# Two classes of landed scatters instead of four, and fewer stated waits, in the expert stage of an attention and routed-FFN kernel

## The chip, the cores and the metric

The kernel runs on 1 core of one Trainium2 chip. The metric is the device time of one execution in microseconds (us). The engines are PE (TensorE, matmuls), DVE (VectorE), ACT (ScalarE), POOL (GpSimd, which here issues the indirect DMAs) and SP (SyncE, which here issues all direct DMAs and does the waiting for them). They run side by side and meet only through semaphores: an instruction or a DMA adds to one, and another engine waits until it has reached a value.

## The reference

```
xn = layernorm(x)                                # x: 16 x 512 tokens of 256
out = x + attention(xn) + ffn(xn)
attention: Q, K = elu(xn Wq' + bq) + 1, elu(xn Wk' + bk) + 1;  V = xn Wv' + bv
           KV = K' V per batch;  context = Q KV / (Q . (sum K + 1e-6));  context Wo' + bo
ffn:       scores = sigmoid(xn gate');  group-limited top 4 of 16 experts, weights scaled by 2.5
           sum over the token's 4 experts of weight * (silu(xn up_e) @ down_e)
           + silu(xn shared_up) @ shared_down
```

So 8192 tokens go to 4 experts each: 32768 token rows, sorted by expert.

## The kernel before

Stage 1 goes over the 16 batches. It computes attention, the shared FFN and the routing, and POOL scatters each token's row into a table in DRAM, `rows_by_expert`. A row there has two halves of 272 words (`RW`): the first holds the normalised row and its weights, the second is the running sum that becomes the output.

Stage 2, the expert stage, works on `UNITS` = 143 units of 256 rows of one expert (`UR`), of which the last few are spare. Each unit goes through these steps, with the names that the rows show:

- SP, `load_rows` (L425): loads the unit's first halves into one of 8 buffers (parts of `xn` and `x_in`). It waits only for the buffer.
- SP, `load_sums` (L434 and L435): loads the second halves into `f_y` (part of `xn`), which other units may have written before. How many earlier units must have landed is known only at run time. The plan at the end of stage 1 (on DVE, `plan_rows`) writes it into a table: column 0 the first row, column 1 the expert, columns 2 to 1 + `CLS` the count for each class, one more for the first 8 units.
- PE, `turn_rows` (L1447): 4 transposes; ACT (L699) and DVE (L1246) split the result into a high and a low part (`xt_h`, `xt_l`).
- PE, up (L316, `bank_x`): 6 matmuls; ACT silu (L720, `hid`), ACT high part (L725, `hs_h`), DVE low part (L1269, `hs_l`).
- PE, down (L316, `bank_a` or `bank_y`): 6 matmuls; DVE (L1258) multiplies by the token's weight (`w`, L1243) and adds the sums.
- POOL (L575): two indirect DMAs of 128 rows scatter the unit's sums back, by the row numbers in `f_id` (L1252).

Each engine has one program order, written out by hand. SP alternates rows of unit u with sums of unit u - 3. PE does up(u), turn(u + 2), down(u - 1).

The classes count landed scatters. Scatters may land out of order, so unit u adds 32 (16 for each of its two DMAs) to semaphore `added[u % CLS]`, and POOL lets unit u's scatter start only once the last unit of the same class has landed: `adds_until(u - CLS)`. A count in a class is thus that of a known set of units. Before each load of sums SP waits for all classes in turn, each against a register. The registers come from the table by one load instruction per column for four units (`four_from`, L323), so every fourth unit has `CLS` such loads among its waits. Before the final copy (L452, 8 DMAs of 1024 KB from the table in DRAM to `out`) SP waits the same way (L447). `PRIMED` is the value that each class starts from: four scatters of batch 14 are counted on these semaphores instead of `scattered`.

ACT and PE wait for the engine that makes their input (`fx_done`, `fx_lo`, `fu_done`, `fs_done`) and, with `wait(...)`, for the last reader of the buffer that they overwrite.

Of the kernel before, what the change touches and what calls it, by code (L numbers as in the profile page):

```python
# [8 lines left out]
ALU = mybir.AluOpType  # L9
# [12 lines left out]
def attention_and_routed_ffn(  # L22
# [17 lines left out]
    B, S, D = x.shape  # L40
# [3 lines left out]
    SUB = S // P  # L44
# [20 lines left out]
    PW = D + 2  # L65
    XB = 3
    NB = 3
    CLS = 4
    COLS = 3 + CLS
    PACK = 6  # L70
    WORDS = -(-UNITS // PACK)
# [8 lines left out]
    with ExitStack() as ctx:  # L80
# [9 lines left out]
        def wait(eng, s, value):  # L90
            if value > 0:
                eng.wait_ge(s, value)
# [129 lines left out]
        u_class_i = sb("u_class_i", [P, CLS, 2], U32)  # L222
        u_class_n = sb("u_class_n", [P, CLS, 2], U32)

# [64 lines left out]
        scattered = [sem(f"scattered{i}") for i in range(NB)]  # L289
        added = [sem(f"added{i}") for i in range(CLS)]  # L290
# [9 lines left out]
        CONSTS = 12  # L300
        fours = {}
        BATCH_SCATTERS = 16 * SUB * TOP_K
        PRIMED = 16

        def scatters_until(c):
            return BATCH_SCATTERS * (c // NB + 1)
# [44 lines left out]
        def _(sp):  # L351
# [56 lines left out]
            sp.wait_ge(zeros_stored, 16 * len(zero_rows))  # L408
            sp.wait_ge(attn_ready, SUB * B)
            sp.wait_ge(scattered[(B - 3) % NB], scatters_until(B - 3))  # L410
            sp.wait_ge(scattered[(B - 2) % NB], scatters_until(B - 2) - 16 * CLS)
            for k in range(CLS):
                sp.wait_ge(added[k], PRIMED)

# [43 lines left out]
        def _(pool):  # L458
# [37 lines left out]
            def scatter_first(c, s):  # L496
                G.indirect_dma_start(  # L497
                    out=by_expert[:, :], in_=xn[:, c % NB, s, :], in_offset=None,
                    out_offset=bass.IndirectOffsetOnAxis(ap=slots_now[:, c % NB, s, 0:1], axis=0)
                ).then_inc(added[s] if c == B - 2 else scattered[c % NB], 16)  # L500

            pool.wait_ge(consts_made, CONSTS)
            inverse_root(0)
# [77 lines left out]
        def _(act):  # L581
# [113 lines left out]

            def rows_high(u):
                act.wait_ge(fx_done, u + 1)
                wait(act, fu_done, u - 3)
                S_.copy(f_h[u % 4], A[u % 2][:, :].rearrange("p (c s t) -> p c s t", c=KD, s=2)).then_inc(fx_hi, 1)  # L699

            act.wait_ge(plan_ready, 1)

            def stage(u):
                expert = expert_from(experts, u)
                wait(act, fu_done, u - 3)
                if u == 0:
                    act.wait_ge(c_done, SUB * B)
                    act.wait_ge(set_lo, SH + E)
                S_.copy(f_w[u % 4], we[:, bass.ds(expert, 1), :, 0:UPW].rearrange("p o a b -> p (o a) b")
                        ).then_inc(fw_ready, 1)  # L710
# [5 lines left out]
                rows_high(u)  # L716
            for u in range(UNITS):
                act.wait_ge(fu_done, u + 1)
                wait(act, fh_lo, u - 1)
                S_.activation(f_hid[u % 2], X[u % 2][:, 0:UR], ACT.Silu).then_inc(fs_done, 1)  # L720
                if u + 2 < UNITS:
                    rows_high(u + 2)
                act.wait_ge(fs_done, u + 1)
                wait(act, fd_done, u - 1)
                S_.copy(f_hh[u % 2], f_hid[u % 2]).then_inc(fh_hi, 1)  # L725
                if u + 2 < UNITS:
                    stage(u + 2)

        @block.vector
        def _(dve):  # L730
            V = nc.vector
# [355 lines left out]
            def plan_rows():  # L1087
                wide_u = [P, 2, B + 1, E - 1]
                V.tensor_scalar(u_tab[:, :, 1], u_ended[:, :], 0.0, None, ALU.max)
                V.tensor_tensor(u_before[:, :], u_first[:, :], u_units[:, :], ALU.subtract)  # L1090
                V.scalar_tensor_tensor(out=u_row[:, :], in0=u_in[:, :], scalar=float(UR), in1=u_base[:, :], op0=ALU.mult,
                                       op1=ALU.add)
                V.tensor_scalar(u_over[:, :], u_in[:, :], float(CAP // UR), 0.5, ALU.is_ge, ALU.mult)
                V.tensor_scalar(u_end_row[:, :], u_in[:, :], float(UR), float(UR), ALU.mult, ALU.add)
                plan(V.tensor_tensor(per_batch[:, :, :, 0:E - 1], mine[:, :, 0:E - 1].unsqueeze(2).to_broadcast(wide_u),
                                     so_far_at[:, :, 1:].unsqueeze(1).to_broadcast(wide_u), ALU.mult))
                planned()
                V.tensor_tensor(u_over[:, :], u_over[:, :], u_by[:, :], ALU.mult)
                V.tensor_reduce(u_other[:, :, :], per_batch[:, :, :, 0:E - 1], AX_X, ALU.add)
                plan(V.tensor_tensor(u_end_row[:, :], u_end_row[:, :], u_mine[:, :, B], ALU.min))  # L1100
                planned()
                V.tensor_tensor(u_row[:, :], u_row[:, :], u_fit[:, :], ALU.subtract)
                V.tensor_tensor(u_last[:, :], u_end_row[:, :], u_mine[:, :, B - 1], ALU.is_gt)
                V.scalar_tensor_tensor(out=u_pad[:, :], in0=u_units[:, :], scalar=float(UR), in1=u_other[:, :, B],
                                       op0=ALU.mult, op1=ALU.subtract)
                plan(V.tensor_tensor(u_below[:, :, :], u_mine[:, :, 0:B], u_end_row[:, :].unsqueeze(2)
                                     .to_broadcast([P, 2, B]), ALU.is_lt))
                planned()
                V.tensor_tensor(u_row[:, :], u_row[:, :], u_over[:, :], ALU.add)
                V.tensor_scalar(u_tab[:, :, 2 + CLS], u_last[:, :], float(BATCH_SCATTERS), float(scatters_until(B - 1 - NB)),  # L1110
                                ALU.mult, ALU.add)
                plan(V.tensor_tensor(u_below[:, :, :], u_below[:, :, :], u_other[:, :, 1:], ALU.mult))
                planned()
                V.tensor_tensor(u_row[:, :], u_row[:, :], u_real[:, :], ALU.mult)
                plan(V.tensor_reduce(u_need[:, :], u_below[:, :, :], AX_X, ALU.max))
                planned()
                V.tensor_tensor(u_tab[:, :, 0], u_row[:, :], u_spare[:, :], ALU.add)
                V.tensor_tensor(u_end[:, :], is_end[:, :], u_first[:, :], ALU.mult)
                plan(V.scalar_tensor_tensor(out=u_need_i[:, :], in0=u_need[:, :], scalar=UR - 1.0, in1=u_pad[:, :],
                                            op0=ALU.add, op1=ALU.add))  # L1120
                planned()
                plan(V.tensor_scalar(u_need_n[:, :], u_need_i[:, :], 8, None, ALU.logical_shift_right))
                planned()
                plan(V.tensor_tensor(u_before[:, :], u_before[:, :], u_need_n[:, :], ALU.add))
                planned()
                plan(V.tensor_tensor(u_before[:, :], u_before[:, :], u_real[:, :], ALU.mult))
                planned()
                plan(V.tensor_tensor(u_before[:, :], u_before[:, :], u_end[:, :], ALU.add))
                planned()
                for k in range(CLS):  # L1130
                    last = V.tensor_scalar(u_class_i[:, k], u_before[:, :], float(CLS - 1 - k), None, ALU.add)
                plan(last)
                planned()
                plan(V.tensor_scalar(u_class_n[:, :, :], u_class_i[:, :, :], 2, None, ALU.logical_shift_right))
                planned()
                V.tensor_scalar(u_tab[:, :, 2:2 + CLS].rearrange("p j k -> p k j"), u_class_n[:, :, :], 32.0, float(PRIMED), ALU.mult, ALU.add
                                ).then_inc(plan_made, 1)
# [137 lines left out]
        def _(pe):  # L1275
# [165 lines left out]

            def turn_rows(u):
                pe.wait_ge(rows_loaded[u % RB], 16 * (u // RB + 1))
                wait(pe, fx_lo, u - 1)
                for h in range(KD):
                    for tile in range(2):
                        last = T_.transpose(A[u % 2][:, (2 * h + tile) * P:(2 * h + tile + 1) * P],  # L1447
                                            f_rows[u % RB][:, tile, h * P:(h + 1) * P], ident[:, :])
                last.then_inc(fx_done, 1)
# [5 lines left out]
            for u in range(UNITS + 1):  # L1455
                if u < UNITS:
                    pe.wait_ge(fx_lo, u + 1)
                    pe.wait_ge(fw_ready, u + 1)
                    wait(pe, fs_done, u - 1)
                    split3(X[u % 2][:, 0:UR],  # L1460
                           [(f_w[u % 4][:, 0, h * I:(h + 1) * I], f_w[u % 4][:, 1, h * I:(h + 1) * I],
                             f_h[u % 4][:, h].rearrange("p s t -> p (s t)"),
                             f_l[u % 4][:, h].rearrange("p s t -> p (s t)")) for h in range(KD)]).then_inc(fu_done, 1)
# [43 lines left out]
```

## Time and profile before

| | |
|---|---|
| device time, median of 3 runs | 968.05 us (966.78 to 970.07) |
| span of the profiled execution, first to last instruction | 963.3 us |
| left around that span, if the execution was the median one | 4.75 us |
| expert stage: first load of rows issued | 466.9 us |
| final copy issued, and last of the span | 928.3 us, 963.3 us |

The page of the profile gives no total for the profiled execution beside its span, so its own time is taken as the span plus what lies around it. Busy time is the share in which an engine executes. In the lists, an idle time is put down to what ended it: a name of an engine and line is the instruction whose result came last; "issue" is that nothing in the profile was waited for; "remote" or "an unknown queue" is that no releaser was found that fits. SPq is SP's own instruction queue.

### The profile page before, as it was taken

The numbers are of one execution on the slowest core, as the hardware profiler recorded it, in microseconds if no ns is written. First come the engines' busy times: TensorE is split into PE (matmuls) and PEld (weight loads), VectorE is DVE, ScalarE is ACT, GpSimd is POOL, SyncE is SP. The second block draws the span as 40 slices with busy tenths as digits, with TensorE's granted clock in tenths as the row PEclk, the third lists the DMA queues.
The fourth block names the chain that finished last, engine by engine and source line by source line (L and its number), as shares of the span: only waits on it lengthen the run. The fifth ranks groups of instructions, "written<-read, shape, count | busy, mean of one in ns | idle before, by whom it ended". The sixth has DMA issues, their size and how long they took to land.

```text
span 963.3 us, 19900 instructions
## 1 busy us (share of the span) xinstructions
PE 763.9 (79%) x5264; PEld 698.6 (73%) x5264; DVE 700.5 (73%) x2390; ACT 551.7 (57%) x1142; POOL 579.7 (60%) x581
## 2 busy tenths in 40 slices
PE   5999999999999999996477676677767767677660
PEld 4899999999899988886366666666656657577660
DVE  6988988888888898889466566556565656666560
ACT  5777777676677766662255455455454554545450
POOL 1077766666777776666556565656565555556562
PEclk9999999999999999999599999989899898979895
DMA  5245554554444443333699798788878888798889
GB/s 160 88 157 193 187 181 175 188 193 182 149 160 181 147 135 118 119 113 117 193 288 285 237 283 254 240 265 261 248 234 281 272 246 272 234 273 252 261 263 311
DMA packets 142317, 202.16 MB, mean 210 GB/s; under 512 B 16176, under 2 KB 117184, under 8 KB 142208
## 3 DMA queue, kind: packets, MB, share of 16 engines
q1 hardware_dynamic: 114144, 116.47, 41.6%
q0 software_dynamic: 28064, 84.43, 22.9%
q8 instruction: 45, 0.74, 0.3%
q14 instruction: 64, 0.52, 0.2%
HBM read 104.19 MB, written 105.04 MB: 217 GB/s over the span
## 4 chain that ended last, share of the span: by engine, by line
PE 25%; issue 10%; DVE 7%; another core or an unknown queue 3%; ACT 2%; POOL 1%; SPq 1%; DVEq 1%; DMA 1%; POOLq 0%; ACTq 0%
PE bank_x L316 8%; PE bank_a L316 6%; PE bank_a L1447 6%; PE bank_y L316 5%; DVE xn L1258 3%; DVE hs_l L1269 2%; ACT xt_h L699 2%; DVE xt_l L1246 1%; DVE w L1243 0%; POOL rows_by_expert L575 0%; DMA xn<-rows_by_expert 0%; DVEq L1243 0%; POOL rows_by_expert L497 0%; SPq L323 0%
## 5 line engine op out<-in xcount | busy, mean ns | idle before, releaser
L575 POOL DMA_INDIRECT rows_by_expert<-xn,f_id x286 | 278.1, 972 | 196.2 <-issue 73.3
L491 POOL DMA_INDIRECT rows_by_expert<-xn,slots_now x192 | 196.7, 1024 | 123.1 <-PE bank_a L316 58.6
L1246 DVE TENSOR_TENSOR xt_l<-bank_a,xt_h 128x512 fp32r<-128x512 f32 x143 | 98.3, 687 | 113.7 <-ACT xt_h L699 96.0
L699 ACT CAST xt_h<-bank_a 128x512 fp32r<-128x512 f32 x143 | 83.8, 586 | 101.9 <-PE bank_a L1447 57.1
L720 ACT ACTIVATE hid<-bank_x 128x256 f32<-128x256 f32 x143 | 55.1, 385 | 123.9 <-PE bank_x L316 79.4
L316 PE MATMUL bank_a<-we,hs_h 128*128 x288 | 67.5, 328 | 68.3 <-DVE hs_l L1269 41.9
L316 PE MATMUL bank_y<-we,hs_h 128*128 x284 | 67.2, 330 | 65.9 <-DVE hs_l L1269 46.3
L316 PEld LDWEIGHTS bank_a<-we,hs_h 128*128 128x128 f32 x288 | 49.1, 206 | 82.0 <-issue 82.0
L316 PEld LDWEIGHTS bank_y<-we,hs_h 128*128 128x128 f32 x284 | 49.2, 209 | 79.4 <-issue 79.1
L316 PE MATMUL bank_y<-ws,hs_h 128*128 128x256 f32 x512 | 94.4, 282 | 1.4 <-DVE hs_l L998 1.4
L316 PE MATMUL bank_x<-xt_h,ws 128*128 128x512 f32 x256 | 92.1, 401 | 0.0
L497 POOL DMA_INDIRECT rows_by_expert<-xn,slots_now x64 | 80.3, 1254 | 17.9 <-issue 14.2
L316 PEld LDWEIGHTS bank_y<-ws,hs_h 128*128 128x128 f32 x512 | 80.9, 188 | 4.4 <-DVE hs_l L998 1.6
L316 PE MATMUL bank_y<-ws,hs_l 128*128 128x256 f32 x256 | 72.3, 282 | 0.0
L1258 DVE SCALAR_TENSOR_TENSOR xn<-bank_a,w,xn 128x256 f32<-128x256 f32 x144 | 62.6, 475 | 12.6 <-PE bank_y L316 7.3
L316 PE MATMUL bank_x<-xt_h,k_h 128*128 128x256 f32 x288 | 70.1, 304 | 0.5 <-issue 0.5
L316 PE MATMUL bank_x<-xt_h,k_l_p 128*128 128x256 f32 x284 | 68.1, 301 | 0.0
L1258 DVE SCALAR_TENSOR_TENSOR xn<-bank_y,w,xn 128x256 f32<-128x256 f32 x142 | 61.6, 474 | 3.9 <-PE bank_a L316 1.8
L652 ACT ACTIVATE k_f<-bank_a,minus_one 128x256 f32<-128x256 f32 x64 | 30.4, 474 | 57.6 <-issue 41.5
L1269 DVE TENSOR_TENSOR hs_l<-hid,hs_h 128x256 fp32r<-128x256 f32 x143 | 59.6, 416 | 1.3 <-issue 1.3
L725 ACT CAST hs_h<-hid 128x256 fp32r<-128x256 f32 x143 | 59.6, 417 | 0.1
L1447 PE MATMUL bank_a<-ident,xn 128*128 128x128 f32 x288 | 48.1, 295 | 10.4 <-DMA xn<-rows_by_expert 10.4
(289 smaller groups left out, 2418.7 us busy)
## 6 DMA issues: line engine op xcount, KB each, us to landing
xn<-rows_by_expert SPq DMA_DIRECT2D x215, 272.0 KB
x_in<-rows_by_expert SPq DMA_DIRECT2D x71, 272.0 KB
rows_by_expert<-spare SPq DMA_DIRECT2D x22, 544.0 KB
x_in<-in_L_attn_x_dram SPq DMA_DIRECT2D x16, 512.0 KB
out_dram<-rows_by_expert SPq DMA_DIRECT2D x8, 1024.0 KB
rows_by_expert<-xn,f_id POOLq DMA_INDIRECT x286
rows_by_expert<-xn,slots_now POOLq DMA_INDIRECT x256
w_raw<-in_L_ffn_expert_up_dram SPq DMA_DIRECT2D x32, 64.0 KB
```

The costliest lines, as they stand in the source:

```text
L316: last = nc.tensor.matmul(dst, a, b, start=start and k == 0, stop=stop and k == n - 1, skip_group_check=mixed)
L491: G.indirect_dma_start(out=half_rows[:, :], in_=xn[:, c % NB, s, 0:RW], in_offset=None, out_offset=bass.IndirectOffsetOnAxis(ap=slots_now[ ...
L497: G.indirect_dma_start(out=by_expert[:, :], in_=xn[:, c % NB, s, :], in_offset=None, out_offset=bass.IndirectOffsetOnAxis(ap=slots_now[:, ...
L575: G.indirect_dma_start(out=half_rows[:, :], in_=f_y[u % YB][:, tile], in_offset=None, out_offset=bass.IndirectOffsetOnAxis(ap=f_id[:, u % ...
L652: S_.activation(k_f[:, s, :], A[s][:, 0:D], ACT.Exp, bias=minus_one[:, 0:1])
L699: S_.copy(f_h[u % 4], A[u % 2][:, :].rearrange("p (c s t) -> p c s t", c=KD, s=2)).then_inc(fx_hi, 1)
L720: S_.activation(f_hid[u % 2], X[u % 2][:, 0:UR], ACT.Silu).then_inc(fs_done, 1)
L725: S_.copy(f_hh[u % 2], f_hid[u % 2]).then_inc(fh_hi, 1)
L1246: V.tensor_tensor(f_l[u % 4], A[u % 2][:, :].rearrange("p (c s t) -> p c s t", c=KD, s=2), f_h[u % 4].bitcast(F32), ALU.subtract).then_inc ...
L1258: last = V.scalar_tensor_tensor(out=y, in0=f_dn[u % 2][tile][:, 0:D], scalar=w2[:, u % 4, tile:tile + 1], in1=y, op0=ALU.mult, op1=ALU.add)
L1269: V.tensor_tensor(f_hl[u % 2], f_hid[u % 2], f_hh[u % 2].bitcast(F32), ALU.subtract).then_inc(fh_lo, 1)
L1447: last = T_.transpose(A[u % 2][:, (2 * h + tile) * P:(2 * h + tile + 1) * P], f_rows[u % RB][:, tile, h * P:(h + 1) * P], ident[:, :])
```

## The change

Four things are edited.

`CLS` goes from 4 to 2. With it the table has 5 columns instead of 7, `PRIMED` is 32 instead of 16, unit u adds to `added[u % 2]`, and POOL's scatter of unit u waits for unit u - 2 to have landed instead of u - 4. SP waits for 2 classes per unit instead of 4 and loads 2 count columns per four units instead of 4.

ACT loses four waits per unit: for `fu_done` ahead of `rows_high` and of `stage`, for `fh_lo` ahead of the silu, for `fd_done` ahead of `hs_h`. PE loses two: for `fx_lo` ahead of the transposes and for `fs_done` ahead of up. No compute instruction and no DMA is added or taken away.

```diff
-    CLS = 4
+    CLS = 2
-        PRIMED = 16
+        PRIMED = 16 * SUB // CLS
@@ sync
-            sp.wait_ge(scattered[(B - 2) % NB], scatters_until(B - 2) - 16 * CLS)
+            sp.wait_ge(scattered[(B - 2) % NB], scatters_until(B - 2) - 16 * SUB)
@@ gpsimd, scatter_first
-                ).then_inc(added[s] if c == B - 2 else scattered[c % NB], 16)
+                ).then_inc(added[s % CLS] if c == B - 2 else scattered[c % NB], 16)
@@ scalar
             def rows_high(u):
                 act.wait_ge(fx_done, u + 1)
-                wait(act, fu_done, u - 3)
             def stage(u):
                 expert = expert_from(experts, u)
-                wait(act, fu_done, u - 3)
...
                 act.wait_ge(fu_done, u + 1)
-                wait(act, fh_lo, u - 1)
                 S_.activation(f_hid[u % 2], X[u % 2][:, 0:UR], ACT.Silu).then_inc(fs_done, 1)
...
                 act.wait_ge(fs_done, u + 1)
-                wait(act, fd_done, u - 1)
                 S_.copy(f_hh[u % 2], f_hid[u % 2]).then_inc(fh_hi, 1)
@@ vector, plan_rows
-                plan(V.tensor_scalar(u_class_n[:, :, :], u_class_i[:, :, :], 2, None, ALU.logical_shift_right))
+                plan(V.tensor_scalar(u_class_n[:, :, :], u_class_i[:, :, :], CLS.bit_length() - 1, None,
+                                     ALU.logical_shift_right))
@@ tensor
             def turn_rows(u):
                 pe.wait_ge(rows_loaded[u % RB], 16 * (u // RB + 1))
-                wait(pe, fx_lo, u - 1)
...
                     pe.wait_ge(fw_ready, u + 1)
-                    wait(pe, fs_done, u - 1)
```

On SP, at the first loads of sums of the expert stage (L323 loads a table column into registers, the ISA rows of L435 wait and form the address), the order changes so, with - for before and + for now:

```order
 L323 TENSOR_LOAD q_f [waits added0]
-L323 TENSOR_LOAD q_f [waits added1]
-L323 TENSOR_LOAD q_f [waits added2]
-L435 ISA [waits added3]
+L435 ISA [waits added1]
 L435 DMA xn<-rows_by_expert 128x2x272
 L323 TENSOR_LOAD q_f x2
 L425 ISA [waits scattered0]
 L425 DMA x_in<-rows_by_expert 128x2x272
-L435 ISA [waits added0,added1,added2,added3]
+L435 ISA [waits added0,added1]
 L435 DMA xn<-rows_by_expert 128x2x272
```

Two table loads with their waits have gone from every fourth unit, and two bare waits from each of the others; all DMAs stand where they stood.

On POOL, at the scatters of units 2 and 3, before:

```order
L575 DMA rows_by_expert<-xn,f_id 237568x272 [waits added2,fd_done,id_ready,y_ready]
L575 DMA rows_by_expert<-xn,f_id 237568x272 [waits fu_done]
L575 DMA rows_by_expert<-xn,f_id 237568x272 [waits added3,fd_done,id_ready,y_ready]
L575 DMA rows_by_expert<-xn,f_id 237568x272 [waits fu_done]
L575 DMA rows_by_expert<-xn,f_id 237568x272 [waits added0,fd_done,id_ready,y_ready]
```

and now:

```order
L575 DMA rows_by_expert<-xn,f_id 237568x272 [waits added0,fd_done,id_ready,y_ready]
L575 DMA rows_by_expert<-xn,f_id 237568x272 [waits fu_done]
L575 DMA rows_by_expert<-xn,f_id 237568x272 [waits added1,fd_done,id_ready,y_ready]
L575 DMA rows_by_expert<-xn,f_id 237568x272 [waits fu_done]
L575 DMA rows_by_expert<-xn,f_id 237568x272 [waits added0,fd_done,id_ready,y_ready]
```

The order is the same; the wait for a landed scatter now names the unit two before.

## Rows read from the trace of the kernel before

**Rows 1.** The page: the span.

```profile
span 963.3 us, 19900 instructions
```

**Rows 2.** Windows: expert stage, and final copy alone. Columns are in the first line.

```profile
core 0: us, PE busy (x) PEld busy (x) DVE busy (x) ACT busy (x) POOL busy (x), PEclk, DMA share, GB/s
484.00:925.00 441.00, 309.08 (x2161) 282.49 (x2162) 271.58 (x809) 228.96 (x540) 260.74 (x268) 0.93 0.84 259
...
943.00:963.00 20.00, 0.00 (x0) 0.00 (x0) 0.00 (x0) 0.00 (x0) 3.80 (x4) 0.50 0.98 306
```

**Rows 3.** Waits 484 to 925 us: who waited for whom, total, times, longest.

```profile
ACT xt_h L699 <- PE bank_a L1447: 55.6, 35, 2.5
...
ACT xt_h L699 <- remote: 36.4, 16, 3.9
...
PEld bank_a L1447 <- DMA xn<-rows_by_expert: 1.7, 1, 1.7
PE bank_a L1447 <- DMA xn<-rows_by_expert: 1.5, 1, 1.5
PEld bank_a L1447 <- DMA x_in<-rows_by_expert: 0.9, 2, 0.5
```

**Rows 4.** The chain of waits, 472 to 493 us: start, us, what ran.

```profile
475.72 0.30 SPq L323
476.12 0.30 SPq L323
476.50 0.30 SPq L323
...
479.19 0.37 SPq L435
479.82 0.37 SPq L425
480.67 0.37 SPq L435
...
482.64 0.69 SPq L424
...
485.23 0.30 SPq L323
...
487.77 4.41 DMA xn<-rows_by_expert
492.22 0.66 PE bank_a L1447 x4
```

**Rows 5.** Waits of SP's queue, 484 to 925 us.

```profile
SPq L434 <- DMA rows_by_expert<-xn,f_id: 22.0, 19, 3.6
SPq L323 <- DMA rows_by_expert<-xn,f_id: 6.4, 3, 2.9
```

**Rows 6.** Timeline of SP's DMAs at the end: start, us, what.

```profile
919.14 0.01 SPq L435 DMA_DIRECT2D xn<-rows_by_expert  x1
...
928.29 25.02 SPq L452 DMA_DIRECT2D out_dram<-rows_by_expert  x8
```

**Rows 7.** SP's waits between 919 and 923 us.

```profile
SPq L323 <- DMA rows_by_expert<-xn,f_id: 2.4, 1, 2.4
```

**Rows 8.** Timeline of POOL, three places; in brackets the idle time before.

```profile
710.22 1.13 POOL L575 DMA_INDIRECT rows_by_expert<-xn,f_id  x1 [0.30 <-issue]
...
714.18 0.96 POOL L575 DMA_INDIRECT rows_by_expert<-xn,f_id  x1 [0.30 <-issue]
...
916.90 0.96 POOL L575 DMA_INDIRECT rows_by_expert<-xn,f_id  x1 [0.30 <-issue]
```

**Rows 9.** Timeline of PE and ACT between 563 and 567 us.

```profile
563.40 1.05 PE L1447 MATMUL bank_a<-ident,x_in 128*128 128x128 f32 x4
...
566.52 0.59 ACT L699 CAST xt_h<-bank_a 128x512 fp32r<-128x512 f32 x1 [1.87 <-remote]
```

## The prediction

> **What bounds the kernel now.** I read four views, in this order. First the windows, because the change touches one stage only. Between 484 and 925 us [rows 2] POOL issues 268 scatters, two per unit, so 134 units pass in 441 us, 3.29 us each. No engine is near full in it: PE 309, DVE 272, POOL 261, ACT 229 of 441 us. The 16 DMA engines are busy 0.84 of the time.
>
> Second the waits of that stretch. ACT stands 55.6 us before it splits the turned rows because of PE's transposes, and another 36.4 us with no releaser found [rows 3]. An example of the latter: the four transposes stand at 563.40 and take 1.05 us, and ACT's next split starts only at 566.52 [rows 9]. What is nearly absent is a wait for loaded rows: PE and its weight queue waited 1.7, 1.5 and 0.9 us for them, 4.1 us together. So in the middle of the stage the ring PE, ACT, DVE, PE sets the pace, and SP's loads come ahead of it.
>
> Third the chain of waits at the start of the stage [rows 4]. There it is different. From 475.72 to 487.77 us the chain runs through SP alone (L323, L434, L435, L425), then through the landing of the rows of unit 8 (4.41 us), and only at 492.22 us reaches PE. In these 12 us the kernel does wait for SP's instructions.
>
> Fourth SP's queue. In the middle it waited 22.0 and 6.4 us for landed scatters, 22 times [rows 5]; at the end its last load of sums stands before the first part of the final copy, which starts at 928.29 us [rows 6]. From there to the end of the span, 963.3 us [rows 1], are 35 us, with the DMA engines at 0.98 in the last 20 of them and nothing else going on but 4 scatters [rows 2]. The final copy is bound by the DMA engines; it moves with its start.
>
> **The change part by part.**
>
> SP at the start of the stage. One table load with its wait costs 0.39 us: the loads stand at 475.72, 476.12 and 476.50 [rows 4]. A bare wait costs 0.07 us: from one DMA to the next it is 0.63 us with one wait between them (479.19 to 479.82) and 0.85 us with four (479.82 to 480.67), so 0.22 us for three [rows 4]. Ahead of the rows of unit 8 stand the sums of units 0 to 4. Units 0 and 4 have table loads: two pairs less each, 4 x 0.39 = 1.56 us. Units 1 to 3 lose two bare waits each, 6 x 0.07 = 0.44 us. Together 2.0 us, all on the chain. From below: the rows before unit 8 shift by 0.8 to 1.2 us only, and if the ring has become the bound already at unit 6 or 7, 1.2 us are left; the landing of 4.41 us may grow by what the loads are closer together. From above: some of SP's steps are longer, as the wait at 482.64 with 0.69 us [rows 4]; if one of the removed steps is such a one, it is 2.7 us. I take 2.0 and keep 0.5 to 2.7.
>
> About the table load the Trainium skill ("DMA: Bandwidth & Descriptors", section "Latency and other measured facts") gives a floor of about 600 ns. The trace shows 0.30 us for three of them [rows 4], so here the trace decides against the page; by the page's figure the four pairs would bring 2.7 us instead of 1.56, an estimate, and the sum would be 1.1 us lower.
>
> SP in the middle. Every four units lose two pairs and six bare waits, 0.78 + 0.44 = 1.2 us, so 134 units about 41 us of SP's time. Cover: the loads come ahead of the ring, and the wait for rows is 4.1 us in all [rows 3]. More than these 4.1 us can't come back directly. I take 0; the time turns into longer waits of SP for landed scatters. Indirectly SP's DMAs shift against the scatters and against the ring; 55.6 + 36.4 us of ACT's waits [rows 3] hang on how such things meet. A twentieth of that, 4.6 us either way, is my estimate of what this may do; I take 0.
>
> SP at the end. The last load of sums waits for a landed scatter eight units back, then come the waits of that unit (four table waits, one of them behind it) and four more before the copy. Two and two of them go, 4 x 0.07 = 0.3 us, on the path, because the copy starts right behind. At least 0.1, at most 1.1 us if the two table loads of the unit two before count as well.
>
> The waits of ACT and PE. Their conditions are true long before: ACT waits for PE or executes most of the time, and what its queue handles meanwhile costs nothing. ACT executes 229 / 134 = 1.7 us of each 3.29 us, PE 2.3 us, so their queues run ahead. The trace does not show the price of such a wait on the path; one per unit at SP's 0.07 us would be 134 x 0.07 = 9 us, none is 0. A loss is excluded, since nothing is issued in their place. I take 0, because before the split ACT idles by whole microseconds [rows 9], and keep 9 as the far end.
>
> The plan on DVE has two small instructions less, some tenths of a microsecond, while POOL still scatters batch 15, which the rows loads wait for. I take 0.
>
> The added wait on POOL. Unit u's scatter now needs unit u - 2 landed. Behind it on POOL stand only later scatters; for them SP waits, 8 units later at most, and for SP the sums of DVE. What a landing takes: SP issued at 919.14 and then waited 2.4 us for the scatter of the unit eight before, whose second DMA stands at 916.90 [rows 6 to 8]. So it landed at 921.55, 4.65 us after its issue. What there is: a unit takes 3.29 us, a pair 6.58 us, less 0.96 + 0.30 us between its two scatters [rows 8], so 5.3 us on average from the second scatter of u - 2 to the first of u. At a tight place it is 3.96 us (710.22 to 714.18) [rows 8]. So on average 0.65 us are to spare, and at tight places POOL starts up to 0.7 us later. POOL has room: 2.5 us of each 3.29 us. The delay reaches only sums that are loaded well ahead. From below 0. From above: should it lengthen each of the 22 waits of SP by 0.7 us, 15 us of waiting, less than the 41 us that SP has won. I take 0 on the path.
>
> The same page of the Trainium skill ("Anatomy of one DMA — SWDGE (gpsimd) path") puts a DMA of this path at 2.0 us plus bytes over 436 GB/s and puts most of the 2 us down to the receipt of the write. For 128 rows of 1088 bytes that is 2.3 us, an estimate, and by it the new wait would never bite. The trace shows twice that, 4.65 us, under load; the sum stays the same by either, but the second makes the wait a real risk.
>
> Sum: 963.3 - 2.0 - 0.3 = 961.0 us of span; with 4.75 us around it 965.75, and since some of the 2.0 us may be swallowed by the ring, I say 966.0 us. The median of the runs shown is 968.05 us, so this is 2 us or 0.2% less.
>
> **The rivals.**
>
> B, SP's relief reaches the path. For it: a wait of SP can stand 0.69 us where others take 0.07 [rows 4], and a queue with fewer instructions is late more seldom. Against it: only 4.1 us of waits for rows [rows 3]. All of them and the start: 966.0 - 4.1 = about 962 us; with one hidden wait of ACT on some units, 961.5 us.
>
> C, the wait on POOL takes over, and the kernel becomes slower. A pair of units can't be faster than 1.27 us plus the landing. At 4.65 us that is 5.9, under 6.58 us. It decides from a landing of 5.3 us on average. At 5.4 us it would be (1.27 + 5.4 - 6.58) / 2 x 134 = 6 us, so 972 us. For it: the DMA engines are at 0.84, and loads issued earlier lie closer to the scatters; in short fast stretches the wait bites already at 4 us. Against it: 0.65 us of spare and loads of sums far ahead.
>
> D, the start brings nothing, since the ring would have waited a few units later anyway: 968 us. For it: the chain changes from SP to the ring just there.
>
> **How the numbers follow.** A measurement of this kernel tells about 0.3%, 2.9 us, from no change. The forecast (A, 966.0 us, its own range 963.5 to 968.5) has 0.45, of which about a third lies below 965.15 us. B has 0.20, all faster. C has 0.18, slower. D has 0.17, mostly no change. That makes faster 0.39, no change 0.41, slower 0.20. The range from 957 us (the 9 us of the hidden waits) to 972.5 us takes in B and the middle of C and leaves out about 0.15.
>
> **What would show it.** Right: the chain between 475 and 492 us is about 2 us shorter, and PE turns the rows of unit 8 near 490.2 us; 72 table loads and 286 waits less on SP; SP's waits for landed scatters grow from 28 us to 40 or more; the middle keeps 3.29 us per unit; the final copy starts 2 to 2.5 us earlier and still takes 35 us. B: a middle below 3.26 us per unit, and no waits for rows at all. C: POOL's idle time put down to a landed scatter of its own (none is there before), with more than 3.32 us per unit. D: PE's turn of unit 8 earlier, but unit 12 at the old time. Wrong altogether I would be if the waits of 55.6 and 36.4 us changed by more than a tenth, for which I have no mechanism.

## The result, and the profile after

The changed kernel takes 975.86 us (median of 17 runs, 966.47 to 980.90), the kernel before 966.31 us (17 runs, 965.22 to 970.07) on the same chip: a ratio of 1.0084, 95% interval 1.0066 to 1.0103. It is slower by 0.8%, where 966.0 us and most likely no loss were forecast; 975.86 us lies outside the range of 957 to 972.5 us. The profiled execution took 980.90 us, the longest of the 17, so the rows below show somewhat more of the loss than the median has.

The page and the windows of the kernel after; the windows answer to [rows 1] and the first of [rows 2]:

```profile
span 978.4 us, 18974 instructions
...
core 0: us, PE busy (x) PEld busy (x) DVE busy (x) ACT busy (x) POOL busy (x), PEclk, DMA share, GB/s
484.00:925.00 441.00, 311.97 (x2122) 283.58 (x2121) 267.99 (x794) 226.45 (x532) 253.93 (x262) 0.90 0.81 253
...
484.00:780.00 296.00, 214.04 (x1471) 193.08 (x1470) 185.19 (x550) 156.69 (x368) 169.85 (x176) 0.92 0.81 254
```

POOL issues 262 scatters in these 441 us instead of 268: 441 / 131 = 3.37 us per unit in place of 3.29. 134 units x 0.08 is 10 us. That is the size of the loss between the medians, 9.6 us. The span of this execution is 15.1 us longer; of that 2.1 us are there before the stage begins (its first load of rows is issued at 469.0 us instead of 466.9) and 2.0 us lie in the final copy, so 11 us fall in the stage. By POOL's own starts the first scatter of unit 4 comes 5.3 us later than before (499.8 instead of 494.5 us) and that of unit 135 12.5 us later (937.7 instead of 925.2): 3 us are lost in the first units and 7 us in the 131 after them.

The waits of the same stretch, answering to [rows 3], with one of POOL that before did not have at all:

```profile
ACT xt_h L698 <- PE bank_a L1443: 35.4, 25, 3.1
POOL rows_by_expert L575 <- DMA rows_by_expert<-xn,f_id: 31.9, 19, 3.0
...
ACT xt_h L698 <- remote: 23.2, 16, 2.5
...
PEld bank_a L1443 <- DMA xn<-rows_by_expert: 15.6, 9, 5.0
PE bank_a L1443 <- DMA xn<-rows_by_expert: 13.8, 8, 4.8
...
PEld bank_a L1443 <- DMA x_in<-rows_by_expert: 9.6, 9, 1.9
```

POOL now stands 31.9 us for landed scatters of its own, and PE stands at loaded rows, which [rows 3] showed with 1.5 us. SP's queue, answering to [rows 5], went from 28 to 113 us of waits for landed scatters:

```profile
SPq L434 <- DMA rows_by_expert<-xn,f_id: 105.7, 58, 7.1
SPq L323 <- DMA rows_by_expert<-xn,f_id: 7.4, 3, 4.8
```

The end, answering to [rows 6], is a timeline of SP's DMAs (start, us, what):

```profile
941.40 23.07 SPq L452 DMA_DIRECT2D out_dram<-rows_by_expert  x8
```

The final copy starts 13.1 us later than before and takes 37.0 us to the end of the span instead of 35.0. At the start of the stage, SP's loads of rows for units 4 and 8 and PE's turns of both; first SP, then PE:

```profile
479.29 0.37 SPq L425 DMA_DIRECT2D x_in<-rows_by_expert  x1
...
485.61 1.12 SPq L425 DMA_DIRECT2D xn<-rows_by_expert  x1
```

```profile
484.05 0.60 PE L1443 MATMUL bank_a<-ident,x_in 128*128 128x128 f32 x4
...
495.93 1.05 PE L1443 MATMUL bank_a<-ident,xn 128*128 128x128 f32 x4
```

And the same four places of the kernel before, SP and PE:

```profile
478.34 0.37 SPq L425 DMA_DIRECT2D x_in<-rows_by_expert  x1
...
481.50 0.66 PE L1447 MATMUL bank_a<-ident,x_in 128*128 128x128 f32 x4 [0.41 <-DMA x_in<-rows_by_expert]
```

SP does get from unit 4 to unit 8 in 6.3 us instead of 9.4 (478.34 to 487.77 [rows 4]), 3.1 us sooner, where 2.0 were forecast. PE does not: 11.9 us between its turns instead of 10.7 (481.50 to 492.22 [rows 4]). The rows of unit 8 no longer hold PE (there is no idle time before its turn now), and something else does. Relative to the first load of rows of the stage, PE turns unit 12 at the same time in both, after 36.5 us before and 36.2 us now.

### The profile page after: what moved, and what is told of

Same layout as the page of the kernel before. It is cut to its first block, busy times and chain, and to the rows that moved or that the text cites. A ratio compares the mean times of both kernels' runs of the same rounds, so it can differ in the third digit from the quotient of the medians.

```text
span 978.4 us, 18974 instructions
## 1 busy us (share of the span) xinstructions
PE 770.0 (79%) x5264; PEld 702.8 (72%) x5264; DVE 701.5 (72%) x2388; ACT 553.0 (57%) x1142; POOL 577.6 (59%) x581
## 4 chain that ended last, share of the span: by engine, by line
PE 16%; issue 11%; DVE 9%; DMA 6%; another core or an unknown queue 3%; ACT 3%; POOL 2%; DVEq 1%; POOLq 0%; SPq 0%; ACTq 0%
PE bank_x L316 5%; DMA rows_by_expert<-xn,f_id 5%; PE bank_a L316 4%; PE bank_y L316 4%; DVE xn L1255 4%; PE bank_a L1443 3%; DVE hs_l L1266 3%; DVE xt_l L1243 1%; DMA xn<-rows_by_expert 1%; POOL rows_by_expert L575 1%; ACT xt_h L698 1%; ACT hid L717 1%; DVE w L1240 1%; ACT hs_h L721 1%
## 5 line engine op out<-in xcount | busy, mean ns | idle before, releaser
L316 PE MATMUL bank_a<-we,hs_h 128*128 x288 | 70.5, 338 | 57.9 <-DVE hs_l L1266 51.2
L316 PEld LDWEIGHTS bank_a<-we,hs_h 128*128 128x128 f32 x288 | 51.7, 217 | 71.5 <-issue 71.5
L1443 PE MATMUL bank_a<-ident,xn 128*128 128x128 f32 x288 | 50.9, 306 | 27.4 <-DMA xn<-rows_by_expert 26.4
L316 PE MATMUL bank_x<-xt_h,k_l_p 128*128 128x256 f32 x284 | 70.3, 308 | 0.0
L1443 PEld LDWEIGHTS bank_a<-ident,xn 128*128 128x128 f32 x288 | 37.8, 157 | 31.0 <-DMA xn<-rows_by_expert 29.5
```

Source lines behind the costliest of these rows:

```text
L316: last = nc.tensor.matmul(dst, a, b, start=start and k == 0, stop=stop and k == n - 1, skip_group_check=mixed)
```

## The experiments

They ran on other chips than the first comparison, and there the kernel before takes 855 to 857 us, not 966. Each was run beside the kernel before on its own chip, and ratios are against that. The times are medians of 4 to 12 executions.

| label | us | ratio to before, 95% interval | us per unit, 484 to 780 us |
|---|---|---|---|
| e1_waits_only | 855.78 | 0.9992 (0.9978 to 1.0006) | 2.55 |
| e2_cls2_only | 963.81 | 1.1235 (1.1190 to 1.1280) | 3.38 |
| e3_gate2 | 951.98 | 1.1119 (1.1089 to 1.1148) | 3.25 |
| e4_sp_padded | 948.65 | 1.1086 (1.1056 to 1.1116) | 3.23 |
| e5_gate3 | 865.21 | 1.0098 (1.0082 to 1.0115) | 2.64 |
| e6_gate1 | 1242.96 | 1.4514 (1.4491 to 1.4537) | 5.24 |
| e7_after_again | 965.98 | 1.1242 (1.1198 to 1.1285) | 3.36 |
| e8_sums3_before | 855.46 | 0.9981 (0.9970 to 0.9993) | 2.55 |
| e9_ring_before | 856.90 | 1.0010 (0.9997 to 1.0024) | 2.54 |
| e10_ring_after | 970.45 | 1.1307 (1.1268 to 1.1346) | 3.40 |
| e11_sums3_after | 963.04 | 1.1236 (1.1210 to 1.1262) | 3.40 |
| e12_ring2_before | 940.73 | 1.1000 (1.0970 to 1.1030) | 3.15 |
| e13_ring2_after | 968.69 | 1.1324 (1.1288 to 1.1360) | 3.33 |

The last column is 296 us over half the count of POOL's scatters in the windows. The three kernels e1, e2 and e3 cut the change into its parts.

**e1_waits_only**: the kernel before without the six waits.

```
-                wait(act, fu_done, u - 3)      (twice)
-                wait(act, fh_lo, u - 1)
-                wait(act, fd_done, u - 1)
-                wait(pe, fx_lo, u - 1)
-                    wait(pe, fs_done, u - 1)
```

> The kernel before, with only the six waits of ACT and PE taken out; four classes stay. Theory G (the wait of POOL's scatter for the unit two before is the cause): as before, 966.3 us, within 2 us, POOL never waits for a landed scatter, SP's waits for landed scatters stay near 28 us. Rival W (without these waits ACT and PE run in another rhythm and this costs the time): as the changed kernel, near 976 us. Rival S (SP's shorter instruction stream costs the time): 966.3 us, like G.

Ratio 0.9992: the six waits are worth nothing that can be measured, with 2 us as the far end of the interval. Its windows row is the measure for what the stage can do on such a chip:

```profile
484.00:780.00 296.00, 253.10 (x1856) 225.18 (x1855) 230.48 (x697) 208.12 (x464) 225.34 (x232) 0.98 0.99 329
```

The DMA engines are at 0.99 and carry 329 GB/s. POOL is at its limit too: it starts 232 scatters in 296 us, and in no run do two scatters start less than 1.26 us apart (0.96 us busy and 0.30 us between), so 232 x 1.26 = 292 of the 296 us are POOL's own spacing. Over units 4 to 135 POOL idles 0.5 us in all beyond these 0.30 us. So on such a chip the ring of engines does not set the pace; POOL's scatters fill 2.53 of the 2.55 us per unit. Neither limit was relieved by itself, so what the DMA engines alone would allow is not known.

**e2_cls2_only**: the changed kernel with the six waits put back, so `CLS = 2` alone.

> The changed kernel with the six waits of ACT and PE put back; two classes. Theory G: as the changed kernel, 973 to 979 us, POOL waits some 30 us for landed scatters and SP 100 us or more. Rival W: back to 966 us. Rival S: 973 to 979 us, like G.

963.81 us, 12.4% over before on its chip: two classes alone bring the loss, so rival W falls. G and S are left.

**e3_gate2**: the kernel before, four classes, SP's program untouched, and one wait more for POOL.

```
                 pool.wait_ge(added[u % CLS], adds_until(u - CLS) if u >= CLS else PRIMED)
+                if u >= 2:
+                    pool.wait_ge(added[(u - 2) % CLS], adds_until(u - 2))
```

> The kernel before, with four classes, the same stream of SP and all waits of ACT and PE; POOL alone waits in addition until the scatter of the unit two before has landed. Theory G: 973 to 979 us, the whole loss, with the lag from a unit's sums to its scatter growing from about 2 to 8 us and SP's waits for landed scatters near 100 us. Rival S: 966 us, since SP's stream is the old one. Rival W: 966 us. If G and S share the loss: 970 us.

952 us: POOL's wait for unit u - 2 alone brings 95 of the 107 us that two classes cost. SP's lighter program, the plan and the classes themselves play no part in these 95 us. The row of its windows beside that of e1:

```profile
484.00:780.00 296.00, 216.55 (x1474) 199.61 (x1475) 190.48 (x554) 164.61 (x369) 176.78 (x182) 0.90 0.83 258
```

**e4_sp_padded**: the changed kernel, but SP loads each of the two count columns twice and waits on each class twice, so that its program is about as long as before.

```
-                for k in range(CLS):
-                    sp.wait_ge(added[k], four_from(..., 2 + k, u, ...))
+                for i in range(2 * CLS):
+                    k = i % CLS
+                    sp.wait_ge(added[k], four_from(..., 2 + k, u, ..., copy))
```

> The changed kernel, in which SP loads each count column twice and waits for each class twice per unit, so that its instruction stream is as long as before; two classes and POOL's wait for the unit two before stay. Theory G: as the changed kernel, 973 to 979 us; SP's waits for landed scatters shorter than 116 us by up to 40 us, since SP comes to them later. Rival S (the shorter stream lets SP's loads collide with the scatters): back to 966 to 968 us.

948.65 us, 15 us faster than e2: the instructions taken from SP cost time instead of bringing any. e3, with SP's full program too, is 12 us faster than e2. So rival S is not what brings the 95 us, but a shorter program of SP adds 12 to 15 us to them.

**e5_gate3 and e6_gate1**: as e3, with u - 3 and with u - 1 in place of u - 2.

> The kernel before, with one wait added: POOL's scatter of unit u also waits for the scatter of unit u-3. Theory G (distance): the two units between leave 2 x 2.56 - 1.26 + 2.56 = 6.4 us from the second scatter of u-3 to the first of u at the pace of the kernel without the wait (2.56 us per unit in the stage), against a landing of about 3.7 us and 0.9 us from landing to start, 4.6 us; so nearly free: within 1% of before, under 866 us where before takes 857. Rival H (any wait of POOL for a landed scatter costs, whatever its distance, since POOL's queue is held by it): about as slow as with u-2, 950 us.

> The kernel before, with one wait added: POOL's scatter of unit u also waits for the scatter of unit u-1, so each unit's two scatters go alone. Theory G: a unit can't be faster than 1.27 us (first scatter to second, and on) less nothing, plus a landing of 3.7 us after the second scatter's start, plus 0.9 us: about 0.96 + 3.7 + 0.9 = 5.5 us a unit against 2.56, 140 units, so about 857 + 410 = 1270 us; at the least 1150 us if the landing falls to 2.8 us because the DMA engines are less busy. Rival H: like the wait for u-2, 950 us.

865 and 1243 us, close to what the distance theory gave (under 866, 1270), and far from its rival's 950. The cost goes by the distance and not by having a wait. e6 shows the wait bare, in its chain of waits (start, us, what):

```profile
607.83 0.99 POOL rows_by_expert L577
608.82 0.30 issue
609.13 2.44 DMA rows_by_expert<-xn,f_id
611.57 0.02 issue
611.59 0.04 POOLq L570
611.63 0.04 issue
611.68 0.04 POOLq L574
611.72 0.73 issue
612.45 0.95 POOL rows_by_expert L577
```

The reader sees two pieces. From the start of the second scatter (607.83) to its landing (611.57) are 3.7 us. Then POOL's queue has the news at once (L570), but its next scatter starts only at 612.45, 0.88 us after the landing. That second piece is what the forecast left out. The profile's spans on POOL are rough, so where exactly a scatter starts, and with it the split into the two pieces, is less sure than their sum.

**e7_after_again**: the changed kernel itself on such a chip.

> The changed kernel itself, beside the others on their chip. If the six removed waits are worth nothing here as well, it takes what the two classes alone took on such a chip, 960 us within 8 us, 11 to 13% over before where before takes 857 us. If the chip is like the first one (before at 966 us), it takes 976 us, 0.8% over.

965.98 us, 12.4% over before. Its POOL timeline (start, us, what, idle time before) has a pattern:

```profile
602.26 0.96 POOL L575 DMA_INDIRECT rows_by_expert<-xn,f_id  x1 [1.50 <-DVE f_id L1249]
603.52 0.96 POOL L575 DMA_INDIRECT rows_by_expert<-xn,f_id  x1 [0.30 <-DMA rows_by_expert<-xn,f_id]
604.79 1.19 POOL L575 DMA_INDIRECT rows_by_expert<-xn,f_id  x1 [0.31 <-issue]
606.28 0.96 POOL L575 DMA_INDIRECT rows_by_expert<-xn,f_id  x1 [0.30 <-issue]
609.06 0.96 POOL L575 DMA_INDIRECT rows_by_expert<-xn,f_id  x1 [1.81 <-DVE f_id L1249]
...
615.89 0.95 POOL L575 DMA_INDIRECT rows_by_expert<-xn,f_id  x1 [2.08 <-DVE xn L1255]
...
622.68 0.96 POOL L575 DMA_INDIRECT rows_by_expert<-xn,f_id  x1 [2.05 <-DVE xn L1255]
```

Four scatters, two units, go close together, then POOL idles 1.5 to 2.1 us until the first unit of the group has landed. The groups start at 602.26, 609.06, 615.89 and 622.68: 6.8 us for two units. The releaser named is mostly DVE's `f_id` or `xn`, and it is the wrong one: by the semaphore events the landing of u - 2 comes 0.86 us ahead of the start, at each of the four. e1 at the same place has no such gaps, and its scatters stand 1.27 us apart without end:

```profile
600.01 0.96 POOL L575 DMA_INDIRECT rows_by_expert<-xn,f_id  x1 [0.30 <-DVE f_id L1248]
601.27 0.96 POOL L575 DMA_INDIRECT rows_by_expert<-xn,f_id  x1 [0.30 <-issue]
602.53 0.96 POOL L575 DMA_INDIRECT rows_by_expert<-xn,f_id  x1 [0.30 <-DVE f_id L1248]
603.80 0.96 POOL L575 DMA_INDIRECT rows_by_expert<-xn,f_id  x1 [0.30 <-PE bank_y L316]
```

So a rule can be written: distance d in units, time for them = 1.26 (first to second scatter) + L (start of the second scatter to its landing) + 0.88. The table takes units 4 to 135 from the semaphore events, those whose scatter starts under 1.05 us after the landing that it waits for:

```
kernel           d  such units  mean L  by the rule, us  measured  rule / d  all units
e6_gate1         1  132 of 132   3.12     5.26             5.30      5.26      5.30
e3_gate2         2   91 of 132   4.32     6.46             6.49      3.23      3.26
e4_sp_padded     2   84 of 132   4.26     6.40             6.45      3.20      3.25
e2_cls2_only     2   73 of 132   4.50     6.64             6.68      3.32      3.36
e7_after_again   2   72 of 132   4.63     6.77             6.77      3.39      3.37
e5_gate3         3   34 of 132   5.82     7.96             8.04      2.65      2.65
```

The measured time of such units agrees with the rule by construction, since they were picked by the third piece. The test is in the last two columns: the rule over d against the pace of all these units, from the start of unit 4 to that of unit 135. They differ by 0.05 us at most. With d = 2 the units that are not in the count are nearly all the second of a group, which follows at once.

The idle time agrees too. What POOL idles beyond 0.30 us ahead of these units is 103 us in e7, 96 in e2 and 86 in e3, where the kernels lose 109, 107 and 95 us. The granted clock is no rival: it is 0.93 in e7 and 0.98 in e1, but e12 and e13 below have 1.00 and 0.99 and still differ by 28 us.

Why a lighter SP makes it worse is not shown. The landings that are waited for take 4.50 to 4.63 us in e2 and e7 and 4.26 to 4.32 in e3 and e4, but they are picked by being waited for: over all units the means are 4.13 and 4.13 against 4.10 and 4.08 us, hardly apart.

**e11_sums3_after**: the changed kernel with `SUMS_AHEAD = 3`. Does the lateness need SP's queue to reach PE?

> The changed kernel (966 us on such a chip) with SP loading the sums three units ahead in place of four, so that it needs a scatter one unit older to have landed. Theory Q (a scatter that starts late after its wait makes SP stand at the load of sums, with the loads of rows behind it, and PE then waits for the rows): with 3.4 us more room the waits of PE for rows shrink, and the unit goes from 3.37 us toward the bound of the pair, (1.26 + 4.15 + 0.86) / 2 = 3.14 us: 935 to 955 us. Rival R (the pair alone bounds it, and SP's queue adds nothing): 960 to 970 us, no change. Against both, sums that come late for DVE: over 975 us.

963.04 against 965.98 us, 1.1236 against 1.1242 by the kernel before on each one's chip: R, no change. The waits only changed place. First e7, then e11, waits from 484 to 780 us:

```profile
PEld bank_a L1443 <- DMA xn<-rows_by_expert: 57.0, 36, 4.2
...
DVE f_id L1249 <- DMA xn<-rows_by_expert: 23.8, 28, 2.8
```

```profile
DVE f_id L1249 <- DMA xn<-rows_by_expert: 80.0, 69, 4.2
...
PEld bank_a L1443 <- DMA xn<-rows_by_expert: 16.9, 15, 3.1
```

PE's waits for rows fall and DVE's for sums rise, at the same pace. They are followers of POOL's pair and not a cause; I had taken them for one.

**e8_sums3_before**: the same in the kernel before, with the six waits out.

> The kernel before with four classes, the six waits of ACT and PE out, and SP loading the sums three units ahead in place of four, so SP waits for a scatter of unit u-5+... one unit younger is no longer asked for so early: SP stood 60.2 us in 55 waits of 3.7 us at line 434 in the variant with four. Theory Q (those waits hold back the loads of rows and weights queued behind, and so PE): with 2.56 us more room each, most of the 60 us of waits go, and a part reaches the end: 840 to 852 us where before takes 857. Rival (DMA engines at 0.99 bound the stage anyhow): 855 to 860 us, no change. Against both, if the sums then come late for DVE: over 865 us.

Ratio 0.9981, interval 0.9970 to 0.9993. Theory Q falls here too: POOL's scatters already stand 1.27 us apart with no idle time beyond the 0.30 us but 0.2 us in all, so there is nothing behind SP's waits to win. It is the only kernel of the study whose whole interval lies below 1, by 1 to 2 us, less than the 0.3% that count here.

**e9, e10, e12 and e13**: why only 0.8% on the first chip? The pace before was 3.29 us per unit there and 2.55 here. These four slow the ring on purpose: ACT does each of its two casts per unit twice (e9 from the kernel before, e10 from the changed one) or three times (e12, e13), the extra ones into tiles that nobody reads.

```
+                S_.copy(q_h[:, u % 2, :], A[u % 2][:, :])
                 S_.copy(f_h[u % 4], ...).then_inc(fx_hi, 1)
...
+                S_.copy(q_l[:, u % 2, 0:UR], f_hid[u % 2])
                 S_.copy(f_hh[u % 2], f_hid[u % 2]).then_inc(fh_hi, 1)
```

> The kernel before, with the ring PE, ACT, DVE, PE made slower: ACT copies each unit's turned rows and its hidden rows twice (first to tiles that nobody reads), 0.59 + 0.41 = 1.0 us more per unit. In the variant with the six waits out a unit takes 2.56 us in the stage, of which ACT executes 2.0. All theories: ACT alone then needs 3.0 us per unit, the ring 3.0 to 3.6; so 857 + 138 x (0.45 to 1.0) = 920 to 995 us, 960 as a guess. It stands in for the first chip, where the kernel before took 3.29 us per unit.

> The changed kernel with the same two extra copies of ACT per unit. Theory M (the slower of the two limits counts, ring or POOL's wait for unit u-2, and on the first chip the ring had already used up the time): only 0 to 3% over the kernel before with the same copies, where without the copies it is 12.4% over. Rival N (the losses add, and the first chip differs in how much the wait itself costs): 11 to 12% over it, some 107 us more, 1065 us.

856.90 us: my expectation for e9 was wrong. The second cast of each kind costs nothing, since ACT still fits into the 2.54 us that POOL's scatters take per unit. So this pair told nothing about M and N, except that the loss stayed at 13%. The larger dose:

> The kernel before, with each of ACT's two casts per unit done three times (twice to tiles that nobody reads). With two each, ACT was busy 280 of 296 us in the stage, 2.42 us per unit, and the time stayed 857 us: the ring had more room than thought. One more of each is 0.64 + 0.47 = 1.1 us, so 3.5 us per unit, ACT the bound in all theories: 857 + 138 x (3.5 - 2.55) = 988 us, 970 to 1000. With that the kernel before has about the pace that it had on the first chip (3.29 us per unit) or is a little slower.

> The changed kernel with the same six casts per unit. Theory M (the slower limit counts; where something else has already taken the pace to 3.3 us or more per unit, POOL's wait for u-2 costs little, as on the first chip with 0.8%): 0 to 3% over the kernel before with the same casts. Rival N (the losses add; the first chip differs in the wait itself): 10 to 12% over it, 107 us or so.

The windows of e12 and then of e13:

```profile
484.00:780.00 296.00, 199.85 (x1501) 177.97 (x1500) 200.43 (x560) 296.00 (x752) 179.06 (x188) 1.00 0.85 266
```

```profile
484.00:780.00 296.00, 200.31 (x1464) 176.82 (x1462) 197.64 (x548) 290.34 (x733) 171.81 (x178) 0.99 0.81 251
```

In e12 ACT never stands, 296.00 of 296 us, and bounds the stage at 3.15 us per unit. That is less than the 3.5 expected, and the time of 940.73 us less than 970 to 1000, because casts that follow each other overlap. ACT's timeline in e12 (start, us, what):

```profile
599.50 1.47 ACT L699 CAST q_h<-bank_a 128x512 fp32r<-128x512 f32 x1
599.99 1.48 ACT L700 CAST xr_h<-bank_a 128x512 fp32r<-128x512 f32 x1
600.46 1.49 ACT L701 CAST xt_h<-bank_a 128x512 fp32r<-128x512 f32 x1
600.94 1.32 ACT L727 CAST q_l<-hid 128x256 fp32r<-128x256 f32 x1
601.25 1.32 ACT L728 CAST xr_l<-hid 128x256 fp32r<-128x256 f32 x1
...
602.66 1.49 ACT L699 CAST q_h<-bank_a 128x512 fp32r<-128x512 f32 x1
```

Each is recorded with 1.3 to 1.5 us, but they start 0.48 and 0.31 us apart, so a further pair costs 0.79 us and not 1.1; the unit is 3.16 us (599.50 to 602.66). The same count gives e9 3.15 - 0.79 = 2.36 us of ACT per unit, under the 2.54 that POOL's scatters take.

With the change the time is 968.69 us, 28 us or 3.0% more and not 109 us. M holds and N falls: the slower of two limits counts. The pace of the changed kernel is 3.33 to 3.40 us per unit in all its forms but the padded one (3.23); what it costs is the distance from the pace before to that. The pace before on the fast chips is taken from e1, as the kernel before was not profiled there. 134 units x (3.36 - 2.55) = 109 us on the fast chips (965.98 - 856.56 = 109.4 measured), x (3.33 - 3.15) = 24 us behind ACT (28.0 measured), x (3.36 - 3.29) = 9 us on the first chip (9.6 measured; by the starts of units 4 and 135 the pace is 3.34 there, which gives 7 us).

## Why the prediction was wrong

**The step that failed** is "The added wait on POOL ... I take 0 on the path". Landing was put at 4.65 us, room at 5.3 us, so 0.65 us to spare. What was missing is the 0.88 us between landing and the next scatter's start, seen in e6. With it 5.53 us stand against 5.3, nothing is to spare, and rival C's own formula gives (1.27 + 4.65 + 0.88) / 2 = 3.40 us per unit against 3.29: 134 x 0.11 = 15 us, so 981 us. Measured are 975.86. Rival C was the right mechanism with one term too few, and got 0.18.

That this sum comes so near is in part luck. The 4.65 us was one landing. The landings that were waited for average 4.63 us in e7, but over all its units the mean is 4.13, and 4.13 + 0.88 us would still have fitted into 5.3.

The same step held that a late scatter reaches only sums that are loaded well ahead. That was the second fault. Room ahead covers a delay that comes now and then. Here the rule limits the rate at which scatters leave, and no room covers a rate: e11 gave more of it, and the waits moved while the pace stayed.

**The spread of landings.** So it is the long landings that hold POOL, and a pair that lost time has no fast successor to win it back. In e7 72 of 132 units were held, about one in each group of two. For the first chip the count can't be given: its trace of the changed kernel has only 1991 of the 4640 landing events of these two semaphores, so the 38 units seen held are a lower bound. What can be said is that POOL's idle time beyond 0.30 us grew there from 96 to 107 us over units 4 to 135, 60 us of it ahead of those 38. My average of 5.3 us of room against one landing hid the spread.

**The waits of ACT and PE**: taken at 0, right; e1 shows at most 2 us, and the far end of 9 us is out.

**SP in the middle**: taken at 0 with 4.6 us either way. e3 and e4 against e2 show a loss of 12 and 15 us by the lighter SP where POOL waits for unit u - 2. So rival B has the sign wrong there; the cause of this part stays open. What such a lighter SP is worth without the wait of POOL was not measured.

**SP at the start**: the mechanism was right, 3.1 us in the place of 2.0, but rival D was right about its worth: PE turned unit 8 no sooner relative to unit 4.

**SP at the end**: 0.3 us can't be seen under the 13 us.

**What was to show it**: C was named by "POOL's idle time put down to a landed scatter of its own, with more than 3.32 us per unit", and that is what the profile after has: 31.9 us and 3.37. SP's waits for landed scatters growing to 40 us or more was to speak for the forecast; they grew to 113, and this sign did not tell the two apart. The sign of being wrong altogether came as well: the waits of 55.6 and 36.4 us became 35.4 and 23.2, both down by over a third. The prediction had no mechanism for that, and no run here isolates it.

The Trainium skill ("DMA: Bandwidth & Descriptors", section "Anatomy of one DMA — SWDGE (gpsimd) path") gives about 2.3 us for such a scatter, an estimate by its 2.0 us plus bytes. Where each unit's scatters go alone, in e6, the landing took 3.12 us, and with the loads of the full stage 4.9 us in e1, both means. With 2.3 us and the 0.88 us of e6 the new wait would fit into 5.3 us, and the page's figure would have let this change pass; the trace decides against it.

**What stays open**: why the kernel before takes 966 us on the first chip and 857 us on three others. On the first chip the DMA engines are at 0.84 to 0.85 in the stage and not at 0.99, and POOL idles 96 us beyond its 0.30 us where it idles 0.5 us in e1. Of SP's steps in the whole program (from one start to the next) 294 take 0.62 to 0.85 us, against 36 in e1 with the same program of SP. ACT's idle time with no releaser found ("remote", 36.4 us in [rows 3]) does not occur in e1's list; whether a result came late there or only its event is missing from the trace is not known. No experiment made this come back on another chip, and slowing ACT only stands in for it. So on the first chip itself the cause of the 9.6 us is inferred: POOL's new waits and its pace there fit it, and e12 and e13 show how a loss of 109 us shrinks to 28 behind a slower stage.

## What to carry to other kernels

Merging counters coarsens what each can tell, and whoever must stay within one count then waits for a younger transfer. Price that as a rate: (issue time of the group + landing + the time from landing to the waiting engine's next start) over the distance in units, with the landing as it is under load, and compare it with the pace of the fastest chip that the kernel runs on; a few tenths of a microsecond of average room are none, as landings vary by more than that. Before taking instructions away from a queue, ask whether it stands on the chain: here a shorter program of SP brought nothing and even cost 12 to 15 us, for a reason not found.

## What the runs showed of the hardware

- In the expert stage two indirect DMAs of 128 rows never start less than 1.26 us apart on POOL, in any run, whatever the share of the DMA engines (0.54 in e6, 0.99 in e1): 0.96 us busy and 0.30 us between.
- From a scatter's landing to the recorded start of the next indirect DMA that waits for it on POOL: 0.86 to 0.88 us, the smallest value in every kernel with the wait, while POOL's queue sees the landing in 0.02 us (chain of e6).
- Casts on ACT without waits between them start 0.48 us (512 columns) and 0.31 us (256) apart and are recorded with 1.3 to 1.5 us each; alone the first takes 0.59 us [rows 9]. So where casts follow each other, the recorded mean is no price for one more.
- The landing of a 128-row scatter goes with the load, as means over all units: 3.12 us with the DMA engines at 0.54 (e6), 4.1 at 0.79 (e7), 4.9 at 0.99 (e1). Single ones took close to 7 us (6.97 in e5).
- The same program takes 966 us on one chip and 855 to 857 us on three others. A change judged on the first alone looked like 0.8%; on the others it is 12.4%.
